# Gated cross-attention with eight experts on one core: another order of the steps of a batch

## What is computed

```
def reference(x, ctx, ...):
    n = layernorm(x)
    # both directions of a cross-attention between n and ctx
    c2s = softmax((n Wq_c + bq_c)(ctx Wk_s + bk_s)^T * s) (ctx Wv_s + bv_s)     # direction 0
    s2c = softmax((ctx Wq_s + bq_s)(n Wk_c + bk_c)^T * s) (n Wv_c + bv_c)       # direction 1
    gate = sigmoid(concat(c2s, s2c) Wg + bg)
    x = x + tanh(g_xattn) * (gate * c2s + (1 - gate) * s2c)
    # top-1 mixture of 8 experts on the normalised rows
    m = layernorm(x)
    p = softmax(m router_w + router_b);  e = argmax(p)
    return x + tanh(g_ffn) * max(p) * (m expert_w[e] + expert_b[e])
```

## Time and profile before

| | |
|---|---|
| timed runs | 1118.87, 1121.82, 1124.72 us; median 1121.82 |
| profiled execution | 1119.28 us, of it 1117.5 us span |
| PE busy | 1071.7 us, 96% of the span |
| DVE, ACT, POOL busy | 70%, 40%, 19% |
| batch 0, up to the first Q of batch 1 | 162.9 us |
| six turns of the loop | about 116 us each |
| granted clock of PE | full, but for the first slices and the stretch from 130 to 150 us |

### The profile page before, as it was taken

One profiled execution on the slowest core, in us unless ns is written; L12 is line 12 of the kernel. 1 busy time (PEld: TensorE's weight loads), 2 busy tenths in 40 slices (PEclk: granted clock), 3 DMA queues, 4 the chain that ended last, 5 costly groups with the idle time before them and its releaser, 6 DMA issues.

```text
span 1117.5 us, 16995 instructions
## 1 busy us (share of the span) xinstructions
PE 1071.7 (96%) x5247; PEld 872.6 (78%) x5247; DVE 776.7 (70%) x1614; ACT 447.2 (40%) x804; POOL 207.6 (19%) x325
## 2 busy tenths in 40 slices
PE   8999599999999999999999999999999999999898
PEld 7877488887888788878887888788887888787676
DVE  7885766667675667667666766686758767888465
ACT  6334514343334334333434333424343426553332
POOL 2000100120012101210121012101120103177564
PEclk9999899999999999999999999999999999999999
DMA  8346122544045304530452245133513354686684
GB/s 302 114 138 203 50 82 61 139 116 123 38 130 145 122 19 131 154 114 36 131 154 63 83 136 144 29 112 104 150 59 95 115 166 136 219 248 205 191 257 125
DMA packets 113889, 143.58 MB, mean 128 GB/s; under 512 B 25434, under 2 KB 58742, under 8 KB 113848
## 3 DMA queue, kind: packets, MB, share of 16 engines
q1 hardware_dynamic: 103680, 117.24, 35.3%
q0 software_dynamic: 7264, 19.20, 5.5%
q10 hardware_dynamic: 2904, 6.63, 1.6%
HBM read 98.94 MB, written 45.93 MB: 130 GB/s over the span
## 4 chain that ended last, share of the span: by engine, by line
PE 72%; DVE 11%; issue 6%; ACT 5%; POOL 3%; SPq 2%; DMA 1%; POOLq 0%; DVEq 0%; ACTq 0%
PE mm L165 49%; PE u L1111 8%; PE u L165 7%; DVE arena L1342 3%; DVE mx L1361 2%; ACT probs L1215 2%; PE tr L165 1%; PE tr L1071 1%; DVE bn_x L1425 1%; PE u L437 1%; ACT arena L1265 1%; PE mm L1937 1%; DVE junk L1442 1%; DVE c2s_pair L1342 1%; PE tr L1155 1%
## 5 line engine op out<-in xcount | busy, mean ns | idle before, releaser
L165 PE MATMUL mm<-arena 128*128 128x512 f32 x1512 | 362.5, 392 | 3.3 <-DVE arena L1342 1.6
L165 PEld LDWEIGHTS mm<-arena 128*128 128x128 f32 x1512 | 280.7, 188 | 66.7 <-ACT probs L1215 5.9
L1111 PE MATMUL u<-arena 128*128 128x512 f32 x768 | 183.2, 390 | 1.8 <-DVE arena L1342 1.6
L165 PE MATMUL mm<-arena,q_pair 128*128 128x512 f32 x768 | 184.1, 394 | 0.0
L1111 PEld LDWEIGHTS u<-arena 128*128 128x128 f32 x768 | 143.4, 188 | 32.4 <-DVE arena L1342 3.0
L165 PEld LDWEIGHTS mm<-arena,q_pair 128*128 128x128 f32 x768 | 141.9, 188 | 29.5 <-issue 0.5
L1558 POOL TENSOR_SCALAR stats<-stats 128x1 f32<-128x1 f32 x32 | 13.9, 434 | 514.0 <-DVE stats L1471 513.8
L165 PE MATMUL mm<-q_pair,arena 128*128 128x512 f32 x360 | 87.3, 392 | 14.1 <-DVE q_pair L1343 14.1
L1342 DVE TENSOR_TENSOR arena<-mm,arena 128x512 fp32r<-128x512 f32 x65 | 44.6, 686 | 79.9 <-ACT arena L1208 79.9
L1215 ACT ACTIVATE probs<-mm,neg_top 128x512 f32<-128x512 f32 x64 | 44.2, 690 | 139.5 <-DVE neg_top L1365 139.5
L1208 ACT ACTIVATE arena<-mm 128x512 fp32r<-128x512 f32 x64 | 38.3, 599 | 152.2 <-PE mm L165 152.1
(11 more groups left out here) (267 smaller groups left out, 1446.6 us busy)
## 6 DMA issues: line engine op xcount, KB each, us to landing
slot_as_f<-in_x_by_columns SPq DMA_DIRECT2D x14, 1024.0 KB, 8.3
slot_as_f<-in_ctx_by_columns SPq DMA_DIRECT2D x8, 1024.0 KB
probs_by_keys<-slot_as_f SPq DMA_DIRECT2D x32, 256.0 KB, 4.0
pairs_as_f<-probs_by_keys SPq DMA_DIRECT2D x8, 1024.0 KB, 6.0
probs_by_keys<-pairs_as_f SPq DMA_DIRECT2D x32, 256.0 KB, 4.2
probs<-probs_by_keys SPq DMA_DIRECT2D x8, 1024.0 KB, 5.3
in_tile<-in_ctx SPq DMA_DIRECT2D x31, 256.0 KB, 6.7
x_rows<-x_tile SPq DMA_DIRECT2D x29, 256.0 KB, 4.3
```

Of the source, the lines that this page charges most:

```text
L165: last = pe.matmul(bank, lhsT(a, c), rhs(b, c), start=start and n == 0, stop=stop and n == C * len(PASSES) - 1)
L1111: last = pe.matmul(u_bank[m][:], v_pair[:, i % 2, a, tile(m)], pt_pair[:, i % 2, p], start=i == 0 and n == 0, stop=i == T - 1 and n == 2)
```

## The change

Only the order of the list changes, with two waits that go with it.

- Next tiles: `n.XS1`, `n.XS2`, `n.XS3` and their `n.XN` come earlier among the steps of direction 1. `n.XD3` goes ahead of U13, `n.CT2` and `n.CT3` behind it. `n.CD3` comes right after KC.
- Scores: PT01 stands behind S13 instead of ahead of it, in every batch.
- Batch 0: the late weights are taken earlier (the last two ahead of U13), SR is moved from the queries to U00, and the fills are issued by WT0 to WT4 instead of WT2 to WT6. ACT waits for them at KC3 (the only `kept` tile that lies in `x_tile`) instead of at KC0.
- SP's broadcast of the statistics waits for U12 through a new semaphore (`third_attended_sums`) instead of for U13.

```diff
-                     Q10 PX03 CD0 CD1 Q11 CD2 SR0 Q12 CD3""") + late(0, 1) + steps("Q13")
+                     Q10 PX03 CD0 CD1 Q11 CD2 Q12 CD3""") + late(0, 1) + steps("Q13") + late(2)
...
-    s += steps("S10") + late(2) + steps("S11 PT00") + late(3) + steps("S12 PX10 PT01 S13 PX11 NP13 PX12")
...
+    s += steps("S10") + late(3) + steps("S11 PT00 S12 PX10 S13 PT01 PX11 NP13 PX12")
...
-    s += steps("n.XN2 n.CT1 U12 n.XD2 n.XS3 n.XN3 n.CT2 p.ID0") + late(12, 13) + load(12, 13, 14)
...
+    s += steps("n.XN3 n.CT1 U12 n.XD2 n.XD3 p.ID0") + late(14, 15) + load(12, 13, 14)
     if last:
         return s + steps_of_the_last_gate(steps, load)
-    s += steps("U13 n.XD3 n.CT3") + late(14, 15) + steps("ND0 ND1 ND2 ND3 n.XA0 n.XA1 n.XA2 n.XA3")
+    s += steps("U13 n.CT2 n.CT3 ND0 ND1 ND2 ND3 n.XA0 n.XA1 n.XA2 n.XA3")
...
-            await_count(sp, waits_passed_sp, u_mm, per_dir(b - 1, 1, C - 1))
+            await_count(sp, waits_passed_sp, u_third, b)
...
+                    if i == T - 2 and d == 1:
+                        last.then_inc(u_third, 1)
...
                         if first:
                             act.wait_ge(c_dotted, T)
-                            lists_filled()
                             act.wait_ge(weights.router_split, 2 * PARTS - 1)
...
                     if i == T - 1:
-                        if not first:
+                        if first:
+                            lists_filled()
+                        else:
...
-                    if 2 <= i < 2 + FILLS:
-                        fill_lists(i - 2)
+                    if i < FILLS:
+                        fill_lists(i)
```

More of the change, by code:

```diff
@@ L521, in steps_of_a_batch @@
                      Q10 PX03 p.BS0 p.NT2 p.M2 Q11 p.NR2 p.MX2 p.BS1 p.NT3 Q12 p.M3 p.LG2 p.NR3 p.MX3 Q13 p.LG3 p.LR3""")
-    s += steps("S10") + late(2) + steps("S11 PT00") + late(3) + steps("S12 PX10 PT01 S13 PX11 NP13 PX12")
[L523 to L528, removed]
-    s += steps("n.XN2 n.CT1 U12 n.XD2 n.XS3 n.XN3 n.CT2 p.ID0") + late(12, 13) + load(12, 13, 14)
+    s += steps("S10") + late(3) + steps("S11 PT00 S12 PX10 S13 PT01 PX11 NP13 PX12")
+    s += steps("V00 PX13 p.BS2 V01 p.BS3 n.CD0 U00") + late(4, 5) + (steps("SR0") if first else []) + load(0)
+    s += steps("V02 PT02 p.RT0 n.CD1 U01") + late(6, 7) + load(1) + steps("n.XS0 V03 PT03 p.RK0 n.XN0 U02") + late(8, 9)
+    s += load(2, 3) + steps("n.XD0 n.CD2 U03") + late(10) + steps("KC0 KC1 KC2 KC3 n.CD3") + table(0) + steps("V10 PT10")
+    s += load(4, 5) + table(1) + steps("CH0 CH1 n.XS1 V11 PT11") + late(11) + load(6) + steps("CH2 CH3 n.XS2") + table(2)
+    s += load(7) + steps("U10 n.XN1") + late(12) + load(8) + steps("n.XS3 V12 PT12") + load(9)
+    s += steps("n.XN2 n.CT0 U11 n.XD1") + late(13) + load(10, 11) + steps("V13 PT13") + fetch(4, 5)
+    s += steps("n.XN3 n.CT1 U12 n.XD2 n.XD3 p.ID0") + late(14, 15) + load(12, 13, 14)
     if last:
         return s + steps_of_the_last_gate(steps, load)
-    s += steps("U13 n.XD3 n.CT3") + late(14, 15) + steps("ND0 ND1 ND2 ND3 n.XA0 n.XA1 n.XA2 n.XA3")
+    s += steps("U13 n.CT2 n.CT3 ND0 ND1 ND2 ND3 n.XA0 n.XA1 n.XA2 n.XA3")
     return s + steps("G00 n.XB0 n.XB1 G01 n.XB2 n.XB3 G02 G03")
@@ L632, in attention_part @@
     probs_turned, turned_stored, probs_loaded = sem("probs_turned"), sem("turned_probs_stored"), sem("probs_by_keys_loaded")
+    u_third = sem("third_attended_sums")
     ct_loaded = sem("ct_loaded")
```

## The result

The changed kernel takes 1102.14 us (median of four runs, 1101.30 to 1103.56), the kernel before on the same chip 1120.87 (1118.87 to 1124.72). The ratio is 0.983, with a 95% interval of 0.980 to 0.986. That is 18.7 us less, where 30 were forecast: 1102 lies just above the range of 1085 to 1101.

A forecast was written before the change was run, and what follows sets the result against it. PE's waits for the attended sums' low part (14.1 us) were taken to bound it. 15.8 + 12.9 + 1.6 + 0.7 - 1.0 = 30.0 us off 1119.28 gave 1089.3, forecast 1090, range 1085 to 1101.

The forecast's parts named there:

- The loop's wait: At the gate's second product in each of six turns: PE's wait for the sums' low part goes wholly, 15.8 us gained.
- What is late next?: Loop step asking what delays the gate once the wait is gone: the sums' first low part is ready 2.5 us early.
- Nothing is added to any engine but one semaphore count: Premise for the whole kernel: no engine gets more work, so the sum is one of waits.
- Batch 0 up to the gate: From V10 to the gate in batch 0: the stops go but for a wait of 0.8, 12.9 us gained.
- The clock: Batch 0's gate: with a wait of only 0.8 ahead of it, the low clock is gone, 1.6 us gained.
- Scores of direction 1: Batch 0, direction 1: one low part goes from ahead of S12's row maximum, 0.7 us gained at U00.
- fills: Batch 0: list fills between direction 1's queries delay the turned probabilities' load; bounds 0 to 3.3 us for PE, 1.0 taken.
- the one by the Trainium skill's rule: Batch 0 rival: fills are mixed wholly into the store, cost nearer 3.3, sum 2.3 us less, 1091.6; chance 0.15 alone.
- PT01 in the other batches: PT01 behind S13 in the other seven batches: between plus 0.5 and minus 0.8 us per batch, taken as 0.
- The broadcast: Gate: statistics land before DVE reaches XA at about 6 us; the new semaphore alone is worth nothing to PE.
- DVE being late once in every batch: Rival in direction 1: moved steps ahead of V11's and V12's low parts lose a microsecond in seven batches, 1096; chance 0.14.
- CD3: Rival ahead of V10 in seven batches: DVE stops for ctx tile 3's load, 1125 us or more; chance 0.03.

The follow-up runs named there:

- after_pad80: The changed kernel with 80 already met waits (40 instructions) put ahead of VectorE's first batch, moving its loop to 331 to 619; 1095.07 us, ratio 0.9766.
- fills_back: The changed kernel with the five list fills issued with WT2 to WT6 again instead of WT0 to WT4; 1097.38 us, ratio 0.9787.
- trim: The changed kernel with 11 fewer VectorE instructions, all repeated waits in the batch loop; 1094.88 us, ratio 0.9766.
- before_pad12: The kernel before with 12 already met waits (6 instructions) put ahead of VectorE's first batch, loop at 293 to 579; 1137.22 us, ratio 1.0138.

## Why the prediction was right and wrong

*The loop's wait, 15.8.* The wait went wholly in all six turns, by the rows of the third turn with the 2.5 us expected. But a turn takes 115.27 and not 113.4: the step that failed is "What is late next?", answered there with nothing, and under it "Nothing is added to any engine but one semaphore count": six wait instructions were added to DVE, four ahead of its loop and two in it. What is late next is DVE at the loop's branch back, five times 115.27 - 113.50 = 1.77, so 8.9 us. after_pad80, where only the loop's place is another, takes 113.51 a turn. The stop does not follow from any wait of the profile before. Without it the gain is 116.07 - 113.50 = 2.57 a turn, so the term itself was sized rightly. Its cause was told too narrowly: the prediction laid the wait on the chain of tile 3, which alone is worth 0.57.

*Batch 0 up to the gate, 12.9.* In after, V10 starts at 108.08 and the gate at 130.56, 22.5 us; before 35.5. The gain is 13.0, with a wait of 0.56 left, where 0.8 was expected. The late weights 14 and 15 are 3.2 of it.

*The clock, 1.6.* Measured 1.54: the gate takes 152.44 - 130.56 = 21.88, and the windows (as above) show full clock in it, against the 0.86 of the earlier trace rows:

```profile
130.00:140.00 10.00, 9.44 (x42) 7.83 (x43) 9.93 (x16) 3.47 (x7) 0.00 (x0) 1.00 0.81 286
140.00:150.00 10.00, 10.00 (x46) 8.29 (x45) 8.54 (x14) 2.67 (x5) 0.00 (x0) 1.00 0.00 0
```

*Scores of direction 1 (+0.7) and fills (-1.0).* Together -0.3 was forecast, and V10 came 4.09 later (108.08 against 103.99). In fills_back V10 starts at 103.73, so the scores give 0.26 and the fills cost 4.35. The step that failed is the 1.0 taken for the fills. Its bound, 4.4 ahead of the load's end and 3.3 at PT00, was nearly right: the load lands 4.67 later than before (81.23 against 76.56), and PT00's copy starts 3.60 later, at 81.28, just beyond the 81 named as the sign. Against the reason for taking little, the third fill does not fall between store and load: all three are issued by 71.2, while SP waits for the store until 73.3. PE then loses 3.14 at V00 (84.55 against 81.41 in fills_back) and 1.3 more up to U00. Of the two views there, the one by the Trainium skill's rule (3.3) was the nearer, and still too small. PT01 in the other batches: taken as 0, it costs 0.16 each.

*The broadcast.* Right: undoing the semaphore changes nothing, and XA starts behind ND without the wait of the earlier trace rows, 5.8 into the gate (6 forecast), as DVE in the third turn shows:

```profile
480.10 0.75 DVE L1401 SCALAR_TENSOR_TENSOR u<-u,bv_col,x_tile 128x512 f32<-128x512 f32 x1
480.76 0.68 DVE L1411 TENSOR_TENSOR slot_as_f<-slot_as_f 128x512 f32<-128x512 f32 x1
```

The sum of 30.0 misses the measured 17.15 by 12.9: 8.9 of it at the branch, 3.8 at the fills and the scores, and 0.2 are left. That so little is left is partly luck: from the gate of batch 7 to the end the five kernels before, after, trim, after_pad80 and fills_back take 165.0 to 168.1 in their profiled executions, and by the medians the stop is worth 7.1 to 7.3 us (after_pad80 and trim) instead of 8.9.

Of the rivals, that of DVE being late once in every batch (1096) had the right engine, but another place in the turn and another mechanism; CD3 stopped nobody. Of the signs, four failed: PE's waits still name L1347, a turn takes 115.27 instead of 113.4, Q00 of batch 1 starts at 152.44 instead of 148.6, and PT00 lies beyond 81. A turn of 113.50 appears in trim and Q00 at 148.09 in fills_back, each without the cost that hid it.

## What to carry to other kernels

Where a loop has about as many instructions on one engine as here (286 to 288 on DVE), count that engine's instructions in and ahead of the loop before and after an edit: a few waits more, even outside of the loop, can add a fixed stop to every turn. The count shows that the loop has moved; whether it now crosses a block's end the trace shows, as "issue" behind the branch, with instruction packets inside the loop. A few instructions fewer in the loop, or more ahead of it, took the stop away here. And transfers put ahead of a store whose end releases a load were paid twice here, in the store and in the load.

## What the hardware showed that was not expected

- The stop at the branch: 2.5 to 2.8 us on DVE in each turn but the first, for a loop of 286 or 288 instructions. For one and the same loop it depends on the place alone. With 286 instructions: 287 to 573 none, 293 to 579 yes. With 288: 291 to 579 and 306 to 594 yes, 331 to 619 none.
- The clock after a wait of one length was not the same. In before, the 2.35 us wait at the gate is followed by full clock (granted 1.00 from 491 to 496, product 3.04). In before_pad12, where a wait of 1.40 at Q02 has come into each turn, a wait of 2.37 is followed by a granted clock of 0.69 over 5 us and a product of 4.62: 1.6 us a turn, more than the new wait itself. That the added wait is the cause was not tried by itself.
- In batch 0 a wait of 3.19 ahead of the gate was followed by full clock (product 3.01), one of 3.35 by the low clock (5.46). What decides between the two was not settled.
